# A two-layer graph kernel: layer 1's projection moved ahead of its neighbour sums, edge values 128 and 192, one foreign-value check per four tiles

## The chip, the cores and the metric

The program runs on one core of one Trainium2 chip. The metric is the device time of one execution in microseconds (us). The core has the matrix engine TensorE (PE; its weight loads are listed apart as PEld), the elementwise engines VectorE (DVE) and ScalarE (ACT), GpSimd (POOL, which here issues gathering DMAs) and SyncE (SP, which issues plain DMAs). Each runs its own instruction list in order; semaphores join them. All DMAs share 16 DMA engines.

## The reference

`x` is 8192x128 float32, `adj` is 8192x8192 int32 with values 0 and 1 (about 0.4% ones, symmetric, ones on the diagonal).

```python
def layer0(x, adj, weight, bias):                 # weight is 256x128
    a = adj.astype(x.dtype)
    deg = jnp.sum(a, axis=1, keepdims=True)
    x1 = a @ x / deg
    return jnp.concatenate([x1, x], axis=1) @ weight + bias
def layer1(x, adj, W, a):                         # graph attention
    h = x @ W.T
    e = (h @ a[:128])[:, None] + (h @ a[128:])[None, :]
    return softmax(where(adj == 0, -inf, e), axis=1) @ h
x = layernorm(x + layer0(x, adj, L0_gnn_weight, L0_gnn_bias))
x = layernorm(x + layer1(x, adj, L1_gnn_W, L1_gnn_a))
```

In layer 1 the row term of `e` cancels in the softmax, so the layer is a product of the 0/1 matrix with rows weighted by exp of the column term.

## The kernel before

The adjacency matrix (268 MB) is read once. It comes in 64 tiles of 128 rows, each as two halves of 2 MB, each half as two indirect DMAs that POOL issues (L1144). `adj_in` has three half slots, so half n is asked for when half n-3 has been converted (`load_half`). ACT converts a half from int32 to fp8 (`convert`, L452), DVE transposes it in 32-bit words (`transpose_half`, L751 and L754) into `edgesT` (two tiles deep), and TensorE contracts the tile with all 64 blocks of `x` (`first_layer`: 64 matmuls at L315 with 257 moving columns: a high and a low fp16 part of 128 columns each, and a column of ones for the degree).

Per tile, the sum over neighbours then goes through: DVE divides by the degree (`degree`, `mean_lo`, `mean`), TensorE transposes that mean and the tile of `x` (`transpose_cat`, L579 and L580), ACT copies both to SBUF (`copy_catT`, L458), TensorE multiplies them with the two halves of the 256x128 weight (`project`, L590 and L591), and DVE adds `x + bias` (prepared by POOL, `add_bias`) and normalizes (`residual` to `normed`). The new row tile is transposed (`transpose_x1`, L585) and multiplied with layer 2's weight (`hidden`, L598). In the code the layers are called 0 and 1.

The edges of four tiles are kept, packed as four bits of each byte (`check_and_pack`): tile c of a group of four has its own bit. The same function checks in two halves of 1024 words that no byte holds anything but its edge value (L763). Packed groups are stored to DRAM. From tile 12 on, TensorE also begins layer 2 for the tile at hand over those row blocks whose weighted rows exist already ("bands" of four blocks, `second_layer_inline`): 4(g-1) matmuls with 258 columns for group g. These partial sums are kept in DRAM as well. After tile 63 a second pass loads the packed groups, unpacks one bit per tile (`unpack`) and does the rest of layer 2 (`second_layer`).

The order on each engine is written out by hand: one loop over tiles in each engine's program, with lags (a tile's projection one step behind, its layer norm two behind, its hidden product three behind). Before the loop, `x` is loaded in four quarters by SP and ACT, ACT makes its high part per quarter (L446), DVE the low part (L732), and TensorE starts tile 0 with the first quarter that is there.

Tile numbers below are t = 0 to 63, groups g = t // 4, blocks of `x` in fours j = 0 to 15.

## Time and profile before

| | us |
|---|---|
| median of 3 runs | 1075.53 |
| lowest, highest | 1073.42, 1077.12 |
| the profiled execution | 1073.98 |
| its span in the profile | 1072.3 |

| engine | busy us | share |
|---|---|---|
| PE | 998.3 | 93% |
| PEld | 868.2 | 81% |
| DVE | 728.6 | 68% |
| ACT | 601.0 | 56% |
| POOL | 310.3 | 29% |

The shares are means over stages that differ. In the first half of the span the DMA engines are 90% busy or more in every fortieth of the span, and from then on less and less; PE is at 70 to 80% at first and at 90% or more from the tenth fortieth to the last but one. The mean granted clock of TensorE is 0.993 of full speed.

### The profile page before, as it was taken

The numbers are of one execution on the slowest core, as the hardware profiler recorded it, in microseconds if no ns is written. First come the engines' busy times: TensorE is split into PE (matmuls) and PEld (weight loads), VectorE is DVE, ScalarE is ACT, GpSimd is POOL, SyncE is SP. The second block draws the span as 40 slices with busy tenths as digits, with TensorE's granted clock in tenths as the row PEclk, the third lists the DMA queues.
The fourth block names the chain that finished last, engine by engine and source line by source line (L and its number), as shares of the span: only waits on it lengthen the run. The fifth ranks groups of instructions, "written<-read, shape, count | busy, mean of one in ns | idle before, by whom it ended". The sixth has DMA issues, their size and how long they took to land.

```text
span 1072.3 us, 22059 instructions
## 1 busy us (share of the span) xinstructions
PE 998.3 (93%) x8777; PEld 868.2 (81%) x8777; DVE 728.6 (68%) x1722; ACT 601.0 (56%) x533; POOL 310.3 (29%) x333
## 2 busy tenths in 40 slices
PE   0778888989999999999999999999999999999996
PEld 0566677777888888888888888888888888888885
DVE  4797888888978877777666665555534655656654
...
GB/s 324 422 421 420 402 409 416 416 417 422 407 421 412 417 395 396 385 386 364 357 346 330 336 325 322 318 314 360 83 127 7 19 71 85 85 85 72 26 41 32
DMA packets 51594, 305.36 MB, mean 285 GB/s; under 512 B 6560, under 2 KB 7840, under 8 KB 17952
## 3 DMA queue, kind: packets, MB, share of 16 engines
...
## 4 chain that ended last, share of the span: by engine, by line
PE 81%; DMA 9%; ACT 4%; issue 2%; DVE 2%; POOL 1%; ACTq 0%; DVEq 0%; POOLq 0%
PE ps_agg L315 48%; PE ps_part L315 24%; DMA adj_in<-in_adj_dram,chunk 8%; PE ps_y L315 4%; ACT edges L452 3%; PE ps_y L591 1%; PE ps_y L590 1%; POOL adj_in L1144 1%; DMA x_all<-in_x_dram 1%; PE ps_h L598 1%; DVE edgesT L754 1%; PE ps_catT L579 0%; PE ps_x1T L585 0%; PE ps_catT L580 0%; DVE edgesT L751 0%
## 5 line engine op out<-in xcount | busy, mean ns | idle before, releaser
L315 PE MATMUL ps_agg<-parts,edgesT 128*128 128x257 f16 (+1 forms) x5312 | 616.7, 275 | 34.6 <-DVE edgesT L754 30.9
L315 PEld LDWEIGHTS ps_agg<-parts,edgesT 128*128 128x128 fp8e4 x5312 | 520.6, 98 | 119.2 <-DVE edgesT L754 35.7
L452 ACT ACTIVATE edges<-adj_in 128x4096 fp8e4<-128x4096 int32 x126 | 455.4, 3614 | 32.5 <-DMA adj_in<-in_adj_dram,chunk 31.8
L1144 POOL DMA_INDIRECT adj_in<-in_adj_dram,chunk x256 | 260.9, 1019 | 440.3 <-ACT edges L452 387.5
L315 PE MATMUL ps_part<-parts,edgesT 128*128 128x258 f16 x1664 | 194.6, 273 | 0.0
L315 PEld LDWEIGHTS ps_part<-parts,edgesT 128*128 128x128 fp8e4 x1664 | 162.7, 98 | 22.7
L763 DVE SCALAR_TENSOR_TENSOR stray<-edgesT,stray 128x1024 uint32<-128x1024 uint32 x128 | 158.4, 1238 | 0.5
L522 ACT ACTIVATE std<-mean_var,eps 128x1 f32<-128x1 f32 x64 | 18.9, 295 | 204.0 <-DVE mean_var L977 204.0
L458 ACT ACTIVATE catT<-ps_catT 128x256 f32<-128x256 f32 x64 | 24.6, 384 | 159.2 <-PE ps_catT L580 145.0
L751 DVE STREAM_TRANSPOSE edgesT<-edges 128x512 uint32<-128x512 uint32 x128 | 89.9, 702 | 16.6 <-ACT edges L452 13.4
L315 PE MATMUL ps_part<-parts,packed 128*128 128x258 f16 x836 | 96.4, 273 | 0.0
L315 PEld LDWEIGHTS ps_part<-parts,packed 128*128 128x128 fp8e4 x836 | 81.7, 98 | 11.8
L754 DVE STREAM_TRANSPOSE edgesT<-edges 128x512 uint32<-128x512 uint32 x128 | 85.8, 670 | 3.5 <-ACT edges L487 3.5
L776 DVE SCALAR_TENSOR_TENSOR packed<-edgesT,packed 128x2048 uint32<-128x2048 uint32 (+13 forms) x48 | 73.0, 1521 | 0.0
L825 DVE TENSOR_SCALAR part_lo<-ps_part 128x129 f32<-128x129 f32 x52 | 14.7, 283 | 67.5 <-PE ps_part L315 65.5
L783 DVE RECIPROCAL rcount<-ps_agg 128x1 f32<-128x1 f32 x64 | 10.2, 160 | 60.7 <-PE ps_agg L315 60.6
L1137 POOL TENSOR_TENSOR xb<-x_all,bias 128x128 f32<-128x128 f32 x64 | 47.9, 750 | 1.3
L315 PE MATMUL ps_y<-parts,packed 128*128 128x258 f16 x380 | 45.1, 273 | 0.0
L315 PEld LDWEIGHTS ps_y<-parts,packed 128*128 128x128 fp8e4 x380 | 37.2, 98 | 5.4
L814 DVE RECIPROCAL rstd<-std 128x1 f32<-128x1 f32 x64 | 10.2, 159 | 43.4 <-ACT std L473 43.4
L579 PE MATMUL ps_catT<-ident,agg 128*128 128x128 f32 x64 | 18.2, 285 | 12.8 <-DVE agg L793 11.1
L953 DVE TENSOR_TENSOR part_lo<-ps_agg,adj_in 128x129 f32<-128x129 f32 x26 | 7.6, 291 | 31.4 <-PE ps_agg L315 31.4
...
## 6 DMA issues: line engine op xcount, KB each, us to landing
adj_in<-in_adj_dram,chunk POOLq DMA_INDIRECT x256, 8.8
...
```

Source lines behind the costliest of these rows:

```text
L315: done = eng.matmul(bank[:, 0:cols], rows[:, n // BYTES, n % BYTES, :], moving[:, n, :], start=(n == first), stop=(n == last))
L452: act.activation(edges[:, half, :, :], adj_in[:, n % SLOTS, :, :], ACT.Copy, scale=2.0 if t % GROUP == GROUP - 1 else 1.0, saturate=False) ...
L458: act.activation(catT[:, :], ps_catT[:, 0:2 * P], ACT.Copy).then_inc(s_catTc, 1)
L522: act.activation(std[:, u % 2:u % 2 + 1], mean_var[:, u % 2, 1:2], ACT.Sqrt, bias=eps[:, :])\
L579: pe.transpose(ps_catT[:, 0:P], agg[:, t % 2, :], ident[:, :])
L751: dve.transpose(dst[:, 2 * half], src[:, 0])
L754: dve.transpose(dst[:, 2 * half + 1], src[:, 1]).then_inc(s_trh, 1)
L763: dve.scalar_tensor_tensor(stray[:, :], edgesT[:, t % 2, part * width:(part + 1) * width], every_byte(0xFF ^ EDGE[c]), stray[:, :], ALU.bi ...
L776: dve.scalar_tensor_tensor(word, bits, every_byte(BIT[c]), word, ALU.bitwise_and, ALU.bitwise_or).then_inc(s_pack, 1)
L825: dve.tensor_scalar(part_lo[:, :], ps_part[:, LO:LO + HCOLS], BIT_SCALE[c], None, ALU.mult)\
L1137: pool.tensor_tensor(xb[:, t % 4, :], x_all[:, t, :], bias[:, :], ALU.add).then_inc(s_xb, 1)
L1144: pool.indirect_dma_start(adj_in[:, n % SLOTS, r, :], None, adj_chunks, bass.IndirectOffsetOnAxis(chunk[:, 0:1], 0), element_offset=first_ ...
```

## The change

Layer 1's projection is linear, so it can be applied to `x` before the neighbour sums. Now u = x @ W[0:128] is made first for all 64 blocks, in 16 groups of four: TensorE transposes four blocks (`transpose_x`), ACT copies them (`copy_xT`), TensorE multiplies them (`dense`), ACT and DVE split the result into the high and the low fp16 part (`split_u`, `split_u_lo`). Tile 0's contraction waits for all 16 (`s_lo0`). The contraction is then over u, so its quotient by the degree is already the projected mean.

The other half, v = x @ (W[128:256] + I) + bias, takes in the residual too (`w0_self`). It is made for two groups ahead of the loop (`dense_self`) and for the other 14 at odd tiles 1 to 27 (`late_transpose_x`, `copy_late_xT`, `late_dense_self`), and DVE writes it over `x_all` (`keep_v`). Per tile, `residual_lo` and `residual` then give the row before its norm directly, without a transpose or a product; its lag goes from two steps to one. `transpose_cat`, `copy_catT`, `project` and POOL's `add_bias` are gone.

Edges are converted to 128 in the first three tiles of a group and to 192 in the fourth, and `KEPT` and `FOREIGN` are masks of their fp8 bytes. Packing keeps a tile's own bit and all bits that an edge never has, at the full 2048 words for every group (before, later groups packed fewer words); the check then reads the packed words once per group instead of every tile. The fourth tile's bit is unpacked with a shift and a mask in one instruction. The four chunks of tile 0 are converted inside the loop over the 16 groups, after steps 11, 13, 15 and 16 (`FIRST_AFTER`), and POOL's first adjacency loads wait for the third quarter of `x` instead of the second.

```diff
-    EDGE = [0x38, 0x38, 0x38, 0x40]
-    BIT = [0x08, 0x10, 0x20, 0x40]
-    BIT_SCALE = [2.0 ** -6, 2.0 ** -5, 2.0 ** -3, 1.0]
+    EDGE = [128.0, 128.0, 128.0, 192.0]
+    KEPT = [0x10, 0x20, 0x40, 0x04]
+    FOREIGN = 0x8B
+    UNPACKED = [2.0 ** -5, 2.0 ** -3, 2.0, 2.0 ** -6]
+    BIT_SCALE = [bit / edge for bit, edge in zip(UNPACKED, EDGE)]
...
+        FIRST_AFTER = [11, 13, 15, 16]
+        AHEAD = 2
+        def late_group(t):
+            j = (t + 3) // 2
+            return j if t % 2 == 1 and AHEAD <= j < GROUPS else None
...
+            def copy_xT(j):
+                act.wait_ge(s_xT, j + 1)
+                if 0 <= j - 2 < AHEAD:
+                    act.wait_ge(s_v, j - 1)
+                wait(act, s_u, j - 1)
+                act.activation(xT[:, j % 2, :, :].rearrange("p c i -> p (c i)"), ps_xT[j % 2][:, :], ACT.Copy)\
+                    .then_inc(s_xTc, 1)
+            def split_u(j):
+                act.wait_ge(s_u, j + 1)
+                act.activation(parts0[:, GROUP * j:GROUP * (j + 1), 0:F],
+                               ps_u[j % 2][:, :].rearrange("p (c f) -> p c f", c=GROUP), ACT.Copy, scale=XSCALE)\
+                    .then_inc(s_hi0, 1)
...
+            for j in range(GROUPS + 1):
+                if j < GROUPS:
+                    copy_xT(j)
+                if j > 0:
+                    split_u(j - 1)
+                if j in FIRST_AFTER:
+                    convert_first(FIRST_AFTER.index(j))
...
-                if on(t, 1):
-                    copy_catT(t - 1)
                 if on(t, 3):
                     copy_x1T(t - 3)
+                if late_group(t) is not None:
+                    copy_late_xT(late_group(t))
...
-                if on(t, 2):
-                    deviation(t - 2)
+                if on(t, 1):
+                    deviation(t - 1)
...
+            def dense(j):
+                pe.wait_ge(s_xTc, j + 1)
+                wait(pe, s_lo0, j - 1)
+                for c in range(GROUP):
+                    last = pe.matmul(ps_u[j % 2][:, c * F:(c + 1) * F], xT[:, j % 2, c, :], w0_sb[:, 0, :],
+                                     start=True, stop=True)
+                last.then_inc(s_u, 1)
...
+            def dense_self(j):
...
+                for c in range(GROUP):
+                    last = pe.matmul(ps_v[j][:, c * F:(c + 1) * F], xT[:, j, c, :], w0_self[:, :],
+                                     start=True, stop=True)
+                last.then_inc(s_v, 1)
...
+            def late_dense_self(j):
+                pe.wait_ge(s_xTlc, j - AHEAD + 1)
+                pe.wait_ge(s_vkept, j)
...
             def first_layer(t):
...
-                wait(pe, s_aggr, t - 1)
...
+                if t == 0:
+                    pe.wait_ge(s_lo0, GROUPS)
+                if t == 1:
+                    pe.wait_ge(s_vkept, AHEAD)
+                contract(pe, ps_agg[t % 2], edgesT[:, t % 2, :], parts0[:, :, 0:2 * F + 1],
+                         range(NBLK), 0, NBLK - 1).then_inc(s_agg, 1)
...
             for t in range(TILES):
-                if on(t, 1):
-                    transpose_cat(t - 1)
                 if on(t, 3):
                     transpose_x1(t - 3)
+                if late_group(t) is not None:
+                    late_transpose_x(late_group(t))
                 first_layer(t)
-                if on(t, 1):
-                    project(t - 1)
                 if on(t, 3):
                     hidden(t - 3)
+                if late_group(t) is not None:
+                    late_dense_self(late_group(t))
                 if inline(t):
                     second_layer_inline(t)
...
-            pe.wait_ge(s_aggr, TILES - 1)
-            second_layer(0, range(0, 16))
-            transpose_cat(TILES - 1)
+            pe.wait_ge(s_z, TILES - 1)
             transpose_x1(TILES - 3)
-            second_layer(0, range(16, 36))
-            project(TILES - 1)
+            second_layer(0, range(0, 8))
             hidden(TILES - 3)
             transpose_x1(TILES - 2)
-            second_layer(0, range(36, READY))
+            second_layer(0, range(8, 16))
             hidden(TILES - 2)
+            transpose_x1(TILES - 1)
+            second_layer(0, range(16, 24))
+            hidden(TILES - 1)
+            second_layer(0, range(24, READY))
...
+            pe.wait_ge(s_z, TILES)
+            second_layer(1, range(0, READY))
...
+            def keep_v(j):
+                dve.wait_ge(s_v, j + 1)
+                if j == 0:
+                    dve.wait_ge(s_bias, 16)
+                dve.tensor_tensor(x_all[:, GROUP * j:GROUP * (j + 1), :],
+                                  (ps_v[j] if j < AHEAD else ps_v_late)[:, :].rearrange("p (c f) -> p c f", c=GROUP),
+                                  bias[:, :].rearrange("p (o f) -> p o f", o=1).to_broadcast([P, GROUP, F]),
+                                  ALU.add).then_inc(s_vkept, 1)
...
-            def check_and_pack(t):
+                words_transposed(t, 2 * half)
...
-                width = TW // CHECKS
-                def check(part):
-                    wait(dve, s_check, CHECKS * t + part)
-                    dve.scalar_tensor_tensor(stray[:, :], edgesT[:, t % 2, part * width:(part + 1) * width],
-                                             every_byte(0xFF ^ EDGE[c]), stray[:, :],
-                                             ALU.bitwise_and, ALU.bitwise_or).then_inc(s_check, 1)
-                check(0)
-                words = slice(bands_of(g) * P, TW)
-                bits = edgesT[:, t % 2, words]
-                word = packed[:, g % 2, words]
+                bits, word = edgesT[:, t % 2, :], packed[:, g % 2, :]
                 if c == 0:
                     wait(dve, s_pkst, 16 * (g - 1))
...
+                    wait(dve, s_check, CHECKS * (g - 1))
+                    dve.tensor_single_scalar(word, bits, every_byte(KEPT[c] | FOREIGN), ALU.bitwise_and)\
+                        .then_inc(s_pack, 1)
                 else:
                     dve.wait_ge(s_pack, t)
-                    dve.scalar_tensor_tensor(word, bits, every_byte(BIT[c]), word, ALU.bitwise_and,
+                    dve.scalar_tensor_tensor(word, bits, every_byte(KEPT[c] | FOREIGN), word, ALU.bitwise_and,
                                              ALU.bitwise_or).then_inc(s_pack, 1)
-                check(1)
+            def check(g, part):
+                width = TW // CHECKS
+                dve.wait_ge(s_pack, GROUP * (g + 1))
+                wait(dve, s_check, CHECKS * g + part)
+                dve.scalar_tensor_tensor(stray[:, :], packed[:, g % 2, part * width:(part + 1) * width],
+                                         every_byte(FOREIGN), stray[:, :],
+                                         ALU.bitwise_and, ALU.bitwise_or).then_inc(s_check, 1)
...
+            def residual_lo(t):
                 dve.wait_ge(s_rdeg, t + 1)
...
+                dve.scalar_tensor_tensor(agg_lo[:, 0:F], ps_agg[t % 2][:, LO:LO + F], rcount[:, :], x_all[:, t, :],
+                                         ALU.mult, ALU.add).then_inc(s_aglo, 1)
+            def residual(t):
                 dve.wait_ge(s_aglo, t + 1)
...
+                dve.scalar_tensor_tensor(z[:, t % 2, :], ps_agg[t % 2][:, 0:F], rcount[:, :], agg_lo[:, 0:F],
+                                         ALU.mult, ALU.add).then_inc(s_z, 1)
...
-                if t in (1, 3, 5, 7):
-                    extremes(t // 2)
+                if t in (40, 44, 48, 52):
+                    extremes(t // 4 - 10)
...
+                if c < 3:
+                    dve.tensor_single_scalar(words_of_turn[u % 4][:, words], source[:, words], every_byte(KEPT[c]),
+                                             ALU.bitwise_and).then_inc(s_unp, 1)
+                else:
+                    dve.tensor_scalar(words_of_turn[u % 4][:, words], source[:, words], 1, every_byte(KEPT[c] << 1),
+                                      ALU.logical_shift_left, ALU.bitwise_and).then_inc(s_unp, 1)
...
-            pool.wait_ge(s_x[1], 16 * NQ)
-            for n in range(SLOTS):
+            pool.wait_ge(s_x[2], 16 * NQ)
+            for n in range(2 * TILES):
                 load_half(n)
```

TensorE's list ahead of and around tile 0, before. `ps_small` receives layer 2's weight, transposed.

```order
L563 MATMUL ps_small<-ident,w_sb 128x128
L564 MATMUL ps_small<-a_sb,w_sb 128x1
L315 MATMUL ps_agg<-parts,edgesT 128x257 x64
L579 MATMUL ps_catT<-ident,agg 128x128
L580 MATMUL ps_catT<-ident,x_all 128x128
```

The same place in the changed kernel, from the last three groups of u on (`partial` here holds the copied transposes; `ps_y` and `ps_h` hold u).

```order
L632 MATMUL ps_catT<-ident,x_all 128x128 x4
L639 MATMUL ps_h<-w_sb,partial 128x128 x4
L632 MATMUL ps_x1T<-ident,x_all 128x128 x4
L639 MATMUL ps_y<-w_sb,partial 128x128 x4
L639 MATMUL ps_h<-w_sb,partial 128x128 x4
L676 MATMUL ps_small<-ident,w_sb 128x128
L677 MATMUL ps_small<-a_sb,w_sb 128x1
L345 MATMUL ps_agg<-parts,edgesT 128x257 x64
L654 MATMUL ps_catT<-ident,x_all 128x128 x4
```

Sixteen steps of four transposes and four float32 products now stand ahead of tile 0 (two of them with four products more, for v), and the transposes for a late group behind it.

ACT's list before its first full conversion, before.

```order
L446 ACT_TABLE_LOAD
L446 ACTIVATE parts<-x_all 128x16x128 x4
L487 ACTIVATE edges<-adj_in 128x2048 x4
L490 ACTIVATE w1T<-ps_small 128x129
L452 ACTIVATE edges<-adj_in 128x4096 x2
```

The end of that part in the changed kernel; L542 converts a chunk of tile 0, L512 is the first half of tile 1.

```order
L504 ACTIVATE parts0<-ps_y 128x4x128 [waits u_done]
L542 ACTIVATE edges<-adj_in 128x2048 [waits first_tile_landed1]
L499 ACTIVATE partial<-ps_catT 128x512 [waits u_done,xT_done]
L504 ACTIVATE parts0<-ps_h 128x4x128 [waits u_done]
L499 ACTIVATE partial<-ps_x1T 128x512 [waits u_done,xT_done]
L504 ACTIVATE parts0<-ps_y 128x4x128 [waits u_done]
L542 ACTIVATE edges<-adj_in 128x2048 [waits first_tile_landed2]
L504 ACTIVATE parts0<-ps_h 128x4x128 [waits u_done]
L542 ACTIVATE edges<-adj_in 128x2048 [waits first_tile_landed3]
L554 ACTIVATE w1T<-ps_small 128x129
L512 ACTIVATE edges<-adj_in 128x4096 [waits half_transposed,adj_landed2]
```

The conversions of tile 0, which free the slots that POOL waits for, now stand behind copies that wait for TensorE.

TensorE's list for a tile in the later part of the loop, before (a tile with 11 bands, then the start of the next).

```order
L590 MATMUL ps_y<-w_sb,catT 128x128
L591 MATMUL ps_y<-w_sb,catT 128x128
L598 MATMUL ps_h<-w1T,x1T 128x129
L315 MATMUL ps_part<-parts,edgesT 128x258 x44
L579 MATMUL ps_catT<-ident,agg 128x128
L580 MATMUL ps_catT<-ident,x_all 128x128
L585 MATMUL ps_x1T<-ident,x_all 128x128
L315 MATMUL ps_agg<-parts,edgesT 128x257 x64
```

The same in the changed kernel, over the step from 10 to 11 bands.

```order
L699 MATMUL ps_h<-w1T,x1T 128x129
L345 MATMUL ps_part<-parts,edgesT 128x258 x40
L692 MATMUL ps_x1T<-ident,x_all 128x128
L345 MATMUL ps_agg<-parts,edgesT 128x257 x64
L699 MATMUL ps_h<-w1T,x1T 128x129
L345 MATMUL ps_part<-parts,edgesT 128x258 x44
```

Two transposes and two float32 products of each tile are gone from TensorE there.

## Rows read from the trace of the kernel before

**Rows 1.** Busy time by stage (us; PEclk, DMA share and GB/s last).
```profile
0.00:26.80 26.80, 0.66 (x3) 0.61 (x3) 11.49 (x7) 14.45 (x8) 15.29 (x23) 1.00 0.97 323
54.00:302.50 248.50, 216.45 (x1844) 183.52 (x1844) 213.99 (x398) 203.29 (x159) 119.96 (x115) 0.99 1.01 415
378.00:423.40 45.40, 45.40 (x406) 40.03 (x407) 34.64 (x73) 35.34 (x29) 18.23 (x21) 1.00 0.99 391
423.40:789.40 366.00, 366.00 (x3276) 323.23 (x3274) 226.42 (x501) 240.06 (x194) 110.74 (x129) 1.00 0.83 316
813.10:1072.30 259.20, 250.91 (x2243) 218.92 (x2241) 151.13 (x573) 22.40 (x76) 0.00 (x0) 0.99 0.17 54
```
**Rows 2.** Chain that ended last: start us, us, what; starts of six contractions.
```profile
65.08 7.35 PE ps_agg L315 x64
...
302.53 7.33 PE ps_agg L315 x64
...
334.08 7.34 PE ps_agg L315 x64
...
423.44 7.16 PE ps_agg L315 x64
...
789.37 1.79 PE ps_agg L315 x16
...
813.06 7.16 PE ps_y L315 x64
```
**Rows 3.** Timeline of PE over one late tile: start us, us, instruction.
```profile
745.93 0.27 PE L579 MATMUL ps_catT<-ident,agg 128*128 128x128 f32 x1
...
746.15 0.27 PE L585 MATMUL ps_x1T<-ident,x_all 128*128 128x128 f32 x1
746.26 7.32 PE L315 MATMUL ps_agg<-parts,edgesT 128*128 128x257 f16 x64
753.42 0.38 PE L590 MATMUL ps_y<-w_sb,catT 128*128 128x128 f32 x2
...
753.87 0.39 PE L598 MATMUL ps_h<-w1T,x1T 128*128 128x129 f32 x2
754.09 6.43 PE L315 MATMUL ps_part<-parts,edgesT 128*128 128x258 f16 x56
```
**Rows 4.** Timeline of the first 40 us; idle time and releaser in brackets.
```profile
7.08 1.28 ACT L446 ACT_TABLE_LOAD   x1 [7.08 <-DMA x_all<-in_x_dram]
...
16.72 1.91 ACT L446 ACTIVATE parts<-x_all 128x2048 f16<-128x2048 f32 x1 [1.00 <-DMA x_all<-in_x_dram]
...
27.59 1.91 ACT L487 ACTIVATE edges<-adj_in 128x2048 fp8e4<-128x2048 int32 x1 [0.57 <-DMA adj_in<-in_adj_dram,chunk]
...
30.30 10.18 PE L315 MATMUL ps_agg<-parts,edgesT 128*128 128x257 f16 x64 [11.78 <-DVE edgesT L754]
```
**Rows 5.** The same chain in its first 34 us.
```profile
3.32 10.46 DMA x_all<-in_x_dram
...
16.76 2.40 issue
19.16 8.40 DMA adj_in<-in_adj_dram,chunk
```
**Rows 6.** Groups of instructions by shape: busy us, mean ns | idle before.
```profile
L452 ACT ACTIVATE edges<-adj_in 128x4096 fp8e4<-128x4096 int32 x126 | 455.4, 3614 | 32.5 <-DMA adj_in<-in_adj_dram,chunk 31.8 <-issue 0.3
L763 DVE SCALAR_TENSOR_TENSOR stray<-edgesT,stray 128x1024 uint32<-128x1024 uint32 x128 | 158.4, 1238 | 0.5
L458 ACT ACTIVATE catT<-ps_catT 128x256 f32<-128x256 f32 x64 | 24.6, 384 | 159.2 <-PE ps_catT L580 145.0 <-issue 14.3
L776 DVE SCALAR_TENSOR_TENSOR packed<-edgesT,packed 128x2048 uint32<-128x2048 uint32 x9 | 22.1, 2458 | 0.0
L463 ACT ACTIVATE x1T<-ps_x1T 128x128 f32<-128x128 f32 x64 | 17.4, 272 | 2.0 <-PE ps_x1T L585 2.0
```
**Rows 7.** PE alone in 42 to 48 us: busy, PEclk, DMA share, GB/s.
```profile
42.00:48.00 6.00, 5.27 (x33) 0.72 1.02 422
```

279 lines of the change are left out of this document (150 added, 129 removed).

## The prediction

> **What bounds the kernel now.** I read the busy times by stage first, then the chain that ended last for the starts of the tiles, then the timeline of one late tile and of the first 40 us. The stages show two limits [rows 1]. From 54 to 302.5 us the DMA share is 1.01 at 415 GB/s while PE is busy for 216 of 248 us: the matrix comes in no faster. From 378 us PE is busy without a gap (45.4 of 45.4, then 366 of 366 us) and the DMA share falls to 0.99 and 0.83: there every PE instruction that goes away shortens the run. The last stage, from 813 us, is PE again, in code that the change hardly touches.
>
> The chain gives the tiles' starts [rows 2]: tile 3 at 65.08, tile 25 at 302.53, tile 28 at 334.08, tile 36 at 423.44, the end of tile 63 at 789.37. Tiles 3 to 25 took 10.79 us each (237.45 / 22), tiles 25 to 27 10.52 each, which I take as the DMA's period; tiles 28 to 35 took 11.17 each.
>
> **The steady part: what goes from TensorE.** In a late tile [rows 3] the two transposes that go stand from 745.93 to 746.15, 0.22 us, and the two products of the projection from 753.42 to 753.87, 0.45 us: 0.67 us per tile. The transpose and product for the hidden rows stay. The v products that come in cost four transposes (0.11 each) and four float32 products (0.225 each), 1.34 us at each odd tile from 1 to 27, or 0.67 per tile: up to tile 27 TensorE's work is thus what it was, inside a DMA-bound stretch; from tile 28 it is less.
>
> Tiles 36 to 63: 28 x 0.67 = 18.8 us, all of it on the chain. Tiles 28 to 35: TensorE would need 11.17 - 0.67 = 10.5, just the DMA's period. With stores of packed groups in the same queue (391 GB/s were moved there at 11.3 us per tile [rows 1], so about 4.4 MB per tile, 10.6 us at 419) I take 10.6: 8 x (11.17 - 10.6) = 4.6 us. At the end of the loop the last tile's transposes and projection go (0.67) and some 0.1 to 0.5 us of a wait for them: 0.8. Sum of the gains: 24.2 us.
>
> **What else changes in the loop.** DVE loses 128 checks of 1.24 us (158 us, rows 6) and gets 32 of them back (40 us). Packing at full width costs 2.46 us where narrower groups took less; for the last groups that is up to 2 us more per tile. DVE is busy 226 of 366 us in tiles 36 to 63 [rows 1], or 8.1 of 13.1 us per tile, and loses about as much as it gains there, so this lies beside TensorE. ACT loses a 0.38 us copy per tile. The norm's step is one tile earlier, and ACT's second conversion of a tile stands behind its square root, which waits for DVE's moments, which wait for the sums of the tile before the last transposed one. From those sums on, DVE's row steps (some 1.5 us), the root, a conversion of 3.61 us [rows 6] and two word transposes are about 7 us; TensorE still has more than a tile's 7.3 us contraction ahead of it. Its cover is thin only where PE is not behind, and there the DMA sets the pace. All this I cost at 0; uncovered, it is rival D. The two-operation unpacking of every fourth tile is at most doubled, some 1.2 us more on a DVE that is busy 151 of 259 us [rows 1]: 0.
>
> **The new part ahead of tile 0.** Before, TensorE waits until 30.30 for tile 0 [rows 4], and the adjacency has been streaming since 19 us at the latest [rows 5]. Now every step j costs TensorE 0.44 us of transposes and 0.90 of products at full clock, twice that at 1.2 GHz, and ACT two copies of 512 columns: 272 ns at 128 columns and 384 at 256 [rows 6] give 0.272 + 3 x 0.112 = 0.61 us each. The engines overlap (two banks for each product), so a step costs about 1.38 us at full clock.
>
> Which clock? Tile 0 took 10.18 us for 64 matmuls [rows 4] where a late tile takes 7.32 [rows 3]. The 2.86 us lost mean 5.7 us at half speed, after idling. And after the idle time at 40 us the granted clock is 0.72 on average over 42 to 48 us [rows 7]. So I count about 6 us of 1.2 GHz from the landing of the first quarter at 7.1 us [rows 4], in which steps 0 and 1 pass with their v products, and then full clock. That puts the products of step 3 at 17.7 and, at 1.38 per step, those of step 10 at 27.2. From there the four chunk conversions of tile 0 (1.91 us each, rows 4) stand in ACT's list between the copies and stretch the steps: they end at about 29.7, 33.8, 37.9 and 40.4 us. Tile 0's contraction starts near 41 us, and since TensorE has idled by then it takes 10 us again.
>
> A late tile 0 is no cost in itself; the DMA queue running dry is. POOL asks for half 3 when the second chunk is converted, for half 4 at the fourth, for half 5 and 6 after the conversions of tile 1. Three halves (6.3 MB), x (4.2) and the rest make 10.8 MB; 8.7 MB moved by 26.8 us [rows 1], the other 2.1 MB take 5 us, so the queue was fed up to 31.8 us. The dead time between the issue and a moving transfer is 2.40 us in the chain [rows 5], with 0.2 for POOL 2.6. The gaps are then:
> - at the start, since the first loads wait for x's third quarter: 1.0 us (2.5 us of x are left to cover 3.5 of issue and dead time), so the queue is empty at 32.8;
> - half 3: 33.8 + 2.6 - 32.8 = 3.6 us, done at 41.4;
> - half 4: 40.4 + 2.6 - 41.4 = 1.6 us;
> - half 5 and 6 come in time; half 7 waits for the first half of tile 2, whose conversion stands behind the copy of the late transposes, and these behind tile 0 on TensorE: 0.7 us.
>
> That is 6.9 us. Lost DMA time is not won back before tile 36, since the DMA is the limit up to there. Bounds: 0 if the steps are hidden behind the loads, about 25 if each step runs in series; the value nearest to the rows is that of overlapping steps, and I take 6.9.
>
> The Trainium skill ("DMA: Bandwidth & Descriptors", section Anatomy of one DMA) gives a lone GpSimd DMA a fixed cost of 2.0 us. By that figure the three later restarts would be 0.4 us shorter each and the sum 1.2 us lower; no row before shows a restart from an empty queue, so the trace neither confirms nor denies it.
>
> **Sum.** The profiled execution took 1073.98 us, 1.7 more than its span, and 1.55 less than the median of 1075.53. 1073.98 - 24.2 + 6.9 = 1056.7; I say 1057 us.
>
> **Rivals.**
> - A, TensorE stays at 1.2 GHz through all 16 steps. For it: the clock is low after short idle times [rows 7]. Against it: at that clock TensorE is the slowest of the three and works without a pause, and tile 0 rose to full speed under continuous work. A step is then 2.64 us; step 10's products end at 39, the second chunk is converted at 47, the fourth at 55. The gaps grow by 14.5 us: 1071.
> - B, slower: each step runs in series, because TensorE's product waits for ACT's copy and ACT's split for the product. At full clock 0.44 + 0.61 + 0.90 + 0.61 and some 0.6 for four hand-overs are 3.2 us. The second chunk is then converted at 7.1 + 14 x 3.2 + 3.8 = 56 instead of 33.8, the gaps grow by 22 us: 1079. It decides against the change once that conversion ends later than 51 us (33.8 + 17.3). Against it: a copy for step j stands ahead of the split of step j-1 in ACT's list, and TensorE's transposes for j ahead of the products for j-1.
> - C, more is won: DVE is busy 214 of 248 us in the DMA-bound stretch [rows 1], and tiles 3 to 25 took 0.27 us longer than the period of 10.52. If DVE's checks were behind that, their going gives up to 22 x 0.27 = 6 us: 1051. Against it: the DMA share is 1.01, which leaves no idle time to win.
> - D, it does not do what it says: with DVE's steps in another order, tiles 36 to 63 wait for the transposed words by what TensorE saved. 1056.7 + 18.8 = 1075.5. Against it: 5 us of DVE are idle per tile.
>
> **How the numbers follow.** Forecast 0.55, A 0.15, B 0.08, C 0.14, D 0.05, others 0.03. A measurement of this kernel tells about 0.3% (3.2 us) from no change. The forecast, C, half of A and a little of the rest are faster: 0.81; half of A and D are no change: 0.10; B and a little more are slower: 0.09. The likeliest case alone spans 1051 to 1064 (gaps of 1 to 14 us). The range reaches down to C with 2 us to spare and up past A: 1049 to 1073.
>
> **What would show it.** In the changed profile: TensorE's products for u packed 1.4 us apart after 14 us, or 2.6 (A) or 3.2 (B); tile 0 starting near 41 us; the DMA share falling below 1 between 32 and 44 us and nowhere else ahead of tile 36; a period of 10.5 to 10.6 us up to tile 36 and then 7.5 us plus 0.45 per band, so that tiles 36 to 63 take 347 us and not 366 (D: 366); no wait of TensorE for the transposed words after tile 36. The prediction is wrong if the gaps at the start exceed 14 us, or if the saved TensorE time reappears as waits in the loop.

## The result, and the profile after

The changed kernel takes 1068.0 us (median of 5 runs, 1065.95 to 1069.11) against 1075.53 before: 7.5 us less, ratio 0.9935 [0.9916, 0.9954]. Run again later it took 1068.84 us beside 1074.77, ratio 0.9947 [0.9929, 0.9966]. The forecast was 1057: faster as foretold, but by less than half.

The page of the changed kernel: VectorE is busy 59 us less, TensorE 4.5 us more.

```profile
PE 1002.8 (94%) x8769; PEld 873.2 (82%) x8769; DVE 669.3 (63%) x1591; ACT 598.4 (56%) x512; POOL 251.4 (24%) x269
```

Busy time by stage in the changed kernel (columns as in [rows 1]):

```profile
0.00:26.80 26.80, 17.20 (x121) 16.25 (x122) 7.17 (x11) 10.64 (x19) 7.26 (x19) 1.00 0.92 299
26.80:54.00 27.20, 20.63 (x157) 17.73 (x156) 13.54 (x20) 22.57 (x23) 8.10 (x8) 0.87 0.77 286
54.00:302.50 248.50, 216.64 (x1822) 185.33 (x1821) 170.81 (x339) 200.04 (x141) 89.11 (x90) 0.95 1.01 410
378.00:423.40 45.40, 43.91 (x391) 38.10 (x390) 32.29 (x67) 34.64 (x26) 17.33 (x18) 1.00 1.01 413
423.40:789.40 366.00, 364.52 (x3257) 319.27 (x3255) 235.11 (x464) 245.18 (x183) 101.04 (x107) 1.00 0.87 333
813.10:1066.30 253.20, 244.88 (x2189) 213.66 (x2187) 145.93 (x554) 20.60 (x71) 0.00 (x0) 0.99 0.17 55
```

The third row is the one to look at. Its DMA share is the same 1.01 as before, but it moved 410 GB/s and not 415, at a clock of 0.95 and not 0.99. That stage was to stay as it was.

The best view for a kernel made of equal tiles is the start of each tile's contraction in TensorE's timeline, set against the kernel before. How much later a tile starts than before, in us (one profiled execution each; further rows are those of the experiments):

| kernel | tile 0 | tile 4 | tile 28 | tile 36 | tile 63 | growth 4 to 28 |
|---|---|---|---|---|---|---|
| changed | 14.0 | 8.5 | 13.9 | 11.7 | -5.3 | 5.4 |
| the same again (c1) | 14.8 | 9.6 | 14.4 | 12.2 | -4.8 | 4.8 |
| e5 loads earlier | 16.2 | 10.5 | 14.8 | 12.5 | -4.5 | 4.3 |
| e6 bias early | 19.1 | 13.6 | 17.7 | 15.4 | -1.6 | 4.1 |
| e8 x whole | 15.3 | 10.1 | 14.2 | 14.7 | -2.3 | 4.0 |
| e13 v kept later | 16.9 | 11.6 | 19.4 | 17.1 | 0.1 | 7.8 |
| e12 fill behind six tiles | 15.4 | 9.7 | 15.0 | 12.8 | -4.2 | 5.3 |
| e4 fill behind four tiles | 15.5 | 9.6 | 10.6 | 8.8 | -8.2 | 1.0 |
| e3 chunks early | 15.4 | 7.3 | 9.0 | 6.7 | -10.2 | 1.6 |
| e1 half 1 back | 15.2 | 11.4 | 12.2 | 9.1 | -8.9 | 0.8 |
| e2 hi rows later | 16.7 | 11.2 | 11.5 | 9.3 | -8.7 | 0.4 |
| e14 both orders | 15.4 | 10.5 | 11.5 | 8.5 | -9.5 | 1.1 |
| e10 start and ScalarE | 22.3 | 16.2 | 17.4 | 14.3 | -3.7 | 1.2 |
| e15 four edits | 15.9 | 8.5 | 9.3 | 5.4 | -12.6 | 0.8 |
| e16 four and fill | 15.1 | 7.7 | 8.9 | 4.8 | -13.2 | 1.3 |

In the changed kernel 8.5 us are lost by tile 4, 5.4 more by tile 28; then 2.2 are won up to tile 36, 17.0 up to tile 63 and 0.7 behind it: 6.0 between the two profiled executions (1073.98 and 1068.0). The late tiles come within 1 us of what was foretold; the start and the middle don't. (Of e13 and e16 the profiled execution was the longest of its kernel, of e3, e4 and e15 the shortest; the medians below tell how far to trust a row.)

**The start.** Its timeline in the changed kernel, by engine:

```profile
9.67 1.12 PE L632 MATMUL ps_x1T<-ident,x_all 128*128 128x128 f32 x4 [4.92 <-DMA x_all<-in_x_dram]
...
20.06 1.13 PE L639 MATMUL ps_h<-w_sb,partial 128*128 128x128 f32 x8 [0.85 <-DVE parts L831]
21.46 1.06 PE L639 MATMUL ps_y<-w_sb,partial 128*128 128x128 f32 x8
...
22.79 1.06 PE L639 MATMUL ps_h<-w_sb,partial 128*128 128x128 f32 x8
```

From 20 to 31 us the steps follow each other by 1.33 us (1.38 was forecast). But the first quarter of `x` is there at 9.67, not 7.1, and step 3 (steps are counted from 0) waits 0.85 us for VectorE, which has waited for the bias. ScalarE finishes the second chunk at 37.06 and the fourth at 43.48 (33.8 and 40.4 forecast). The DMA windows around it (the last three columns are the clock, the DMA share and GB/s):

```profile
32.00:34.00 2.00, 0.79 (x7) 0.56 (x6) 0.78 (x2) 2.00 (x4) 0.00 (x0) 1.00 0.63 262
34.00:36.00 2.00, 2.00 (x20) 2.00 (x19) 1.33 (x2) 1.73 (x3) 0.00 (x0) 1.00 0.03 12
36.00:38.00 2.00, 0.79 (x7) 0.55 (x6) 0.71 (x1) 2.00 (x4) 0.67 (x1) 1.00 0.02 4
38.00:40.00 2.00, 1.85 (x17) 1.69 (x17) 1.27 (x2) 1.73 (x4) 1.20 (x2) 1.00 0.55 78
40.00:42.00 2.00, 0.26 (x4) 0.18 (x2) 0.90 (x3) 2.00 (x3) 0.00 (x0) 1.00 0.94 373
42.00:50.00 8.00, 5.72 (x28) 4.07 (x29) 4.48 (x7) 8.00 (x4) 4.36 (x4) 0.57 0.95 320
```

From 32 to 42 us 1.46 MB were moved, 3.5 us of work at 419 GB/s: 6.5 us are lost. From 42 to 50 it is 1.9 us, and 24 GB/s less over the first 26.8 us are 1.5 us. Sum 9.9, where tile 3 starts 9.5 late.

**The middle.** The chain that ended last, in the changed kernel, from one load to another that it delays:

```profile
209.99 12.52 DMA adj_in<-in_adj_dram,chunk
...
222.53 3.63 ACT edges L512
...
226.82 0.68 DVE edgesT L853
...
227.55 8.81 PE ps_agg L345 x64
...
237.47 1.34 PE ps_part L345 x12
238.81 0.11 PE ps_x1T L692
238.92 7.16 PE ps_agg L345 x64
...
247.76 0.45 PE ps_catT L654 x4
...
248.23 0.02 ACT xT_late L491
...
248.72 3.62 ACT edges L512
...
252.60 1.05 POOL adj_in L1261
```

The stage is not bound by the DMA alone. The chain goes through two contractions, since ScalarE's list has the copies of TensorE's transposes ahead of the next conversion, and the next load waits for that conversion. TensorE's side of it:

```profile
223.68 0.60 PE L654 MATMUL ps_catT<-ident,x_all 128*128 128x128 f32 x4
227.55 8.81 PE L345 MATMUL ps_agg<-parts,edgesT 128*128 128x257 f16 x64 [3.27 <-DVE edgesT L853]
```

TensorE idles for 3.27 us, its clock falls, and the contraction takes 8.81 us where 7.33 is usual. What comes of it in ScalarE's timeline and in the windows:

```profile
238.96 0.28 ACT L518 ACTIVATE x1T<-ps_x1T 128x128 f32<-128x128 f32 x1 [2.06 <-PE ps_x1T L692]
239.13 3.61 ACT L512 ACTIVATE edges<-adj_in 128x4096 fp8e4<-128x4096 int32 x1
```
```profile
220.00:224.00 4.00, 4.00 (x38) 3.59 (x36) 2.41 (x6) 3.41 (x4) 1.87 (x2) 1.00 1.03 421
228.00:230.00 2.00, 2.00 (x11) 1.42 (x10) 1.83 (x6) 2.00 (x1) 0.60 (x1) 0.50 1.08 389
238.00:240.00 2.00, 2.00 (x21) 1.76 (x19) 1.79 (x7) 1.04 (x2) 0.84 (x1) 1.00 0.91 328
```

A clock of 0.50 at 228 us is the lower of the two levels. At 238 the DMA moves 328 GB/s with a share of 0.91. Idle times of 2.5 to 4.6 us ahead of a contraction stand in this trace at 65, 97, 139, 162, 183, 227 and 272 us, most of them ahead of tiles 4g + 1; the slow contractions (8.7 to 10.1 us) follow all but the first. In the kernel before the longest idle time of this kind between 60 and 340 us is 1.8 us, and two contractions there take 8.97.

What is new behind a group's end shows in ScalarE's groups: its high part of the weighted rows waits for VectorE 9 times, 10.0 us in sum (0.8 us in the kernel before), and the next conversion stands behind it.

```profile
L537 ACT ACTIVATE parts<-h_row 128x516 f16<-128x516 f32 x16 | 10.2, 638 | 10.1 <-DVE h_row L951 10.0
```

TensorE's waits for transposed words go on behind this stage. These are the contractions of tiles 29, 33 and 37:

```profile
360.02 7.34 PE L345 MATMUL ps_agg<-parts,edgesT 128*128 128x257 f16 x64 [1.70 <-DVE edgesT L853]
403.03 7.33 PE L345 MATMUL ps_agg<-parts,edgesT 128*128 128x257 f16 x64 [1.25 <-DVE edgesT L853]
446.93 7.33 PE L345 MATMUL ps_agg<-parts,edgesT 128*128 128x257 f16 x64 [0.77 <-DVE edgesT L853]
```

### The profile page after: what moved, and what is told of

It reads as the page before. It is cut to its first block, busy times and chain, and to the rows that moved or that the text cites. A ratio compares the mean times of both kernels' runs of the same rounds, so it can differ in the third digit from the quotient of the medians.

```text
span 1066.3 us, 21633 instructions
## 1 busy us (share of the span) xinstructions
PE 1002.8 (94%) x8769; PEld 873.2 (82%) x8769; DVE 669.3 (63%) x1591; ACT 598.4 (56%) x512; POOL 251.4 (24%) x269
## 4 chain that ended last, share of the span: by engine, by line
PE 70%; ACT 12%; DMA 9%; issue 5%; DVE 2%; POOL 1%; ACTq 1%; DVEq 0%
PE ps_agg L345 40%; PE ps_part L345 23%; ACT edges L512 9%; DMA adj_in<-in_adj_dram,chunk 8%; PE ps_y L345 4%; DMA bias<-in_L_gnn_bias_dram 1%; DVE edgesT L853 1%; PE ps_h L699 1%; POOL adj_in L1261 1%; ACT L528 1%; ACT L533 1%; PE ps_y L639 1%; ACT edges L542 0%; ACTq L477 0%; PE ps_x1T L692 0%
## 5 line engine op out<-in xcount | busy, mean ns | idle before, releaser
L512 ACT ACTIVATE edges<-adj_in 128x4096 fp8e4<-128x4096 int32 x126 | 454.6, 3609 | 33.6 <-DMA adj_in<-in_adj_dram,chunk 33.5
L1261 POOL DMA_INDIRECT adj_in<-in_adj_dram,chunk x256 | 249.9, 976 | 496.3 <-ACT edges L512 422.7
L853 DVE STREAM_TRANSPOSE edgesT<-edges 128x512 uint32<-128x512 uint32 x256 | 166.8, 689 | 141.8 <-ACT edges L512 137.5
L345 PEld LDWEIGHTS ps_part<-parts,edgesT 128*128 128x128 fp8e4 x1664 | 162.7, 98 | 22.7
L882 DVE SCALAR_TENSOR_TENSOR packed<-edgesT,packed 128x2048 uint32<-128x2048 uint32 x48 | 109.5, 2282 | 0.0
L518 ACT ACTIVATE x1T<-ps_x1T 128x128 f32<-128x128 f32 x64 | 17.6, 275 | 138.6 <-PE ps_x1T L692 138.6
L889 DVE SCALAR_TENSOR_TENSOR stray<-packed,stray 128x1024 uint32<-128x1024 uint32 x32 | 39.0, 1218 | 0.0
L932 DVE TENSOR_SCALAR part_lo<-ps_part 128x129 f32<-128x129 f32 x52 | 15.1, 290 | 37.3 <-PE ps_part L345 36.8
L699 PE MATMUL ps_h<-w1T,x1T 128*128 128x129 f32 x128 | 24.7, 275 | 0.7 <-ACT x1T L518 0.7
L910 DVE SCALAR_TENSOR_TENSOR z<-ps_agg,rcount,agg_lo 128x128 f32<-128x128 f32 x64 | 22.5, 351 | 2.3
L902 DVE SCALAR_TENSOR_TENSOR agg_lo<-ps_agg,rcount,x_all 128x128 f32<-128x128 f32 x64 | 22.5, 351 | 2.3
L925 DVE TENSOR_SCALAR x_all<-z,mean_var,rstd 128x128 f32<-128x128 f32 x64 | 22.2, 347 | 2.3
```

The source lines that it names most:

```text
L345: done = eng.matmul(bank[:, 0:cols], rows[:, n // BYTES, n % BYTES, :], moving[:, n, :], start=(n == first), stop=(n == last))
L512: act.activation(edges[:, half, :, :], adj_in[:, n % SLOTS, :, :], ACT.Copy, scale=EDGE[t % GROUP], saturate=False).then_inc(s_conv, 1)
L518: act.activation(x1T[:, :], ps_x1T[:, 0:P], ACT.Copy).then_inc(s_x1Tc, 1)
L699: pe.matmul(ps_h[:, 0:HCOLS], x1T[:, :], w1T[:, 0:HCOLS], start=True, stop=True).then_inc(s_h, 1)
L853: return dve.transpose(dst[:, r], src)
L882: dve.scalar_tensor_tensor(word, bits, every_byte(KEPT[c] | FOREIGN), word, ALU.bitwise_and, ALU.bitwise_or).then_inc(s_pack, 1)
```

## The experiments

Theory S: the start is priced by the moments at which the second and the fourth chunk are converted. Theory 1: the order around a group's end uses up the lead in the middle. VectorE now transposes both halves of a tile before it makes the weighted rows, which is new; ScalarE's part of these rows stands ahead of a conversion, which it did before as well. Theory 2: the lower clock after TensorE's idle times is what costs there. Theory 3: the copies, transposes and products for v at odd tiles cost it.

**e1: VectorE's second half goes back behind the weighted rows.**

```diff
                 if on(t, 0) and t > 0:
                     transpose_half(t, 0)
-                    transpose_half(t, 1)
...
                     if t == weighted_at(g):
                         weighted(g)
+                if on(t, 0) and t > 0:
+                    transpose_half(t, 1)
```

> The changed kernel with one line moved on DVE: the second half of a tile is again transposed behind the weighting of a finished group (weighted), as before, and no longer ahead of it. Theory 1 (DVE's order makes ACT wait at every group's end, so a slot of adj_in is freed late and the DMA stream thins out): ACT's waits for h_row (9 times, 10.0 us) go, tiles 12 to 28 start 170 to 172 us apart in sum and not 176.1, and the median falls by 4 to 6 us, to 1062 to 1064. Theory 2 (TensorE's clock falls after the longer idle times before tiles 4g+1, and those tiles take 8.7 to 10.1 us and not 7.3): no change, 1068. Theory 3 (the loss is the copy, transposes and products for v at odd tiles): no change, 1068.

1065.29 us (1064.26 to 1067.39), ratio to before 0.9908 [0.989, 0.9925]. The growth from tile 4 to tile 28 falls from about 5 to 0.8 us, and ScalarE's wait for the weighted rows from 10.0 to 0.8 us. Tiles 12 to 28 took 173.5 us, less of a gain than the 170 to 172 expected, and the time is 1.3 us above the expected range.

**e2: ScalarE's weighted rows behind the conversion.**

```diff
-                for g in range(GROUPS - 1):
-                    if t == weighted_at(g):
-                        weighted_hi(g)
                 if on(t + 1, 0):
                     convert(t + 1, 0)
+                for g in range(GROUPS - 1):
+                    if t == weighted_at(g):
+                        weighted_hi(g)
```

> The changed kernel with one block moved on ACT: the high part of the weighted rows (weighted_hi) is made behind the first conversion of the next tile, not ahead of it; DVE's order is that of the change. Theory 1: ACT's wait for the weighted rows falls into a time in which they are long made, tiles 12 to 28 take 170 to 173 us, the median is 1063 to 1065. Theories 2 and 3: 1068.

1065.43 us (1062.04 to 1071.35), ratio 0.9911 [0.9884, 0.9938]; growth 0.4 us, tiles 12 to 28 in 171.1 us, ScalarE's wait 0.8 us. This edit restores nothing: it is an order that neither kernel had. The work for v is in both e1 and e2 as it was, so theory 3 is not borne out.

**e3: chunks of tile 0 converted earlier.**

```diff
-        FIRST_AFTER = [11, 13, 15, 16]
+        FIRST_AFTER = [6, 8, 10, 12]
```

> The changed kernel with the four chunks of tile 0 converted after steps 6, 8, 10 and 12 instead of 11, 13, 15 and 16. If the hole in the DMA stream from 33 to 41 us is due to when the second and fourth chunk are converted (37.1 and 43.5 us), they are now converted at about 31 and 40 us, the two holes shrink from 8.7 us in sum to about 6, and the median falls by 2 to 3 us to 1065 or 1066. If later stages make good what the start loses, it falls by under 1 us.

1066.74 us (1063.76 to 1067.63), ratio 0.9915 [0.9896, 0.9933]: 1.3 to 2.1 us less than the changed kernel in its two measurements, where 2 to 3 were expected. The second chunk is done at 31.6 and the fourth at 39.9, but tile 4 starts only 1.2 us earlier: half 5 now waits 6.46 us for tile 1's first conversion, which stands behind all steps, and a hole opens at 48 us.

**e4: TensorE kept busy behind tiles 12, 16, 20 and 24.**

```diff
+                if t in (12, 16, 20, 24):
+                    contract(pe, ps_small, edgesT[:, t % 2, :], parts0[:, :, 0:2 * F + 1], range(16), 0, 15)
```

> The changed kernel with 16 more matmuls (1.8 us at full clock) on TensorE in tiles 12, 16, 20 and 24, into a bank that nobody reads, ahead of the idle time after which the clock falls. Theory 2: contractions 13, 17, 21 and 25 take 7.3 us and not up to 10.1, tiles 12 to 28 take 4 to 6 us less, the median is 1062 to 1064. Theories 1 and 3: the contractions may be shorter, but ACT and the DMA set the pace: 1067 to 1069.

1066.12 us (1065.67 to 1068.01), ratio 0.9917 [0.99, 0.9933]; in its trace no idle time above 2 us and no slow contraction after 173 us; growth 1.0 us, tiles 12 to 28 in 170.8 us. ScalarE's wait for the weighted rows is still there, 10.1 us in sum. The trace is as theory 2 foretold, the time lies between the two forecasts. More work on TensorE, and nothing slower.

**c1 and e5: the changed kernel again, and its loads let go at x's second quarter.**

```diff
-            pool.wait_ge(s_x[2], 16 * NQ)
+            pool.wait_ge(s_x[1], 16 * NQ)
```

> The changed kernel itself, once more, as the yardstick of this call, and for a second profile of it. The experiments so far left their loop alone or moved one block, and all took 171 to 173 us from tile 12 to 28 where the first profile of the change has 176.1. If that was the change's own, it is again 175 to 177 us; if it was chance of one execution, it is 170 to 173. The median should be 1066 to 1069.

> The changed kernel with POOL's first adjacency loads behind the second quarter of x again, as before, and not the third. The prediction added up the holes in the DMA stream, so by it the one at 16 to 19 us (about 2 us) is won back: 2 us faster. Theory S (only the times at which the second and the fourth chunk of tile 0 are converted count, because they release the next loads): the queue runs dry 2 us earlier and the hole from 33 us on grows by as much; no change, or 0.5 us slower since x lands later.

1068.84 us (1066.07 to 1071.75) and 1068.92 (1064.81 to 1074.72), ratios 0.9947 [0.9929, 0.9966] and 0.9953 [0.9934, 0.9971]. Tiles 12 to 28 took 175.1 us in c1: the loss is the change's own and no chance of one execution. In e5 the first load went out at 13.3 and not 14.8 to 15.8 us, but the products of step 3 waited 2.19 us (1.59 in c1) and the second chunk was done at 39.3: nothing was won by the hole closed at the front. This agrees with theory S.

**e8: x without its separate first blocks.** Their four DMAs fall away, and the weight goes behind the first quarter.

```diff
-            for a in (2, 3):
-                act.dma_start(x_all[QUAD * a:QUAD * (a + 1), 0:BYTES, :].rearrange("p c f -> p (c f)"),
-                              x_quarters[0, a][:, 0, :]).then_inc(s_xfirst, 16)
-            act.dma_start(w0_sb[:, :, :], w0.rearrange("(c p) f -> p c f", p=P)).then_inc(s_const, 16)
...
-                    first = 1 if s == 0 else 0
+                    first = 0
```

> The changed kernel with the first quarter of x in one piece per 32 rows again (no DMAs for its first block ahead), and the weight behind it. If the late landing of that quarter (9.7 us instead of 7.1) is due to the six DMAs put ahead of it, it lands at 7.1 to 8 us, the chunks are converted 1.5 to 2.5 us earlier and so are all tiles: 1 to 2 us faster. If TensorE's work at the low clock sets the start, the time is the same.

1068.89 us (1066.85 to 1071.59), ratio 0.9948 [0.993, 0.9966]. The first quarter is there at 7.03 us, as the forecast had it, but the products of step 3 then wait 3.67 us for VectorE, which waits for the bias, and the second chunk is done at 38.4. The first blocks' DMAs are neither the gain nor the delay.

**e6: the bias asked for early; e13: needed later.** e6 moves the DMA; e13 leaves it and moves VectorE's first two copies of v:

```diff
             act.dma_start(w0_sb[:, :, :], w0.rearrange("(c p) f -> p c f", p=P)).then_inc(s_const, 16)
+            act.dma_start(bias[:, :], b0.rearrange("(o f) -> o f", o=1).to_broadcast([P, F])).then_inc(s_bias, 16)
```
```diff
-                if 0 < j <= AHEAD:
-                    keep_v(j - 1)
+                if 6 < j <= 6 + AHEAD:
+                    keep_v(j - 7)
```

> The changed kernel with the bias asked for right behind w0 instead of behind x's last quarter, so that VectorE's first copy of v does not wait for it (it waited 4.26 us in the changed kernel, and the split of step 3 behind it held TensorE up for 0.85). If the start is priced by when the second and fourth chunk are converted: both about 0.9 us earlier (36.2 and 42.6 instead of 37.1 and 43.5), 1067.2 where the changed kernel takes 1068.0 to 1068.8. Rival: step 3 then waits as long for x itself, no gain, 1068 to 1069.

> The changed kernel with VectorE's first two copies of v (which need the bias) moved from steps 1 and 2 to steps 7 and 8. No DMA moves. If the wait for the bias held the steps up: none of TensorE's products for u waits at step 3, tile 0 starts 1 to 3 us earlier (near 42.5), the second and fourth chunk are converted near 36 and 42, and the time is 1066 to 1067.5. Rival: the steps then wait for x itself, nothing changes, 1068 to 1069.

e6: 1072.27 us (1067.9 to 1077.47), ratio 0.9973 [0.9954, 0.9992]. Slower than the changed kernel: with this DMA of 64 KB, the same 512 bytes for each of 128 partitions, ahead of it x came later: TensorE's second transposes, the first that need the whole quarter, start at 11.48, and the first load goes out at 18.26. e13: 1070.09 us (1068.33 to 1074.02), ratio 0.9949 [0.9929, 0.9969], no gain. The wait of step 3 is gone, but a pause of 2.7 us comes at step 6, and in e6 one of 2.65. Both expectations failed: the wait for the bias stands in the traces, but nothing is won by taking it away.

**e7: the kernel before with the checks alone** (edges 128 and 192, packing at full width, one check per group; its order and its projection stay).

```diff
-                    check_and_pack(t)
+                    pack(t)
+                if on(t, 1) and (t - 1) % GROUP == GROUP - 1:
+                    check((t - 1) // GROUP, 0)
+                if on(t, 2) and (t - 2) % GROUP == GROUP - 1:
+                    check((t - 2) // GROUP, 1)
```

> The kernel before with one part of the change alone: edges 128 and 192, packing at full width, one check per group on the packed words; the projection, all orders and the start are those of before. If DVE's checks held up the DMA-bound stretch (rival C of the prediction), tiles 3 to 28 take 263 to 265 us instead of 269.0 and the median falls by 3 to 5 us. If DVE was no limit there, 1074 to 1076: no change.

1072.46 us (1070.58 to 1077.35), ratio 0.9978 [0.9959, 0.9997]. Tile 4 starts 2.1 us earlier than before, and tile 63 2.3 earlier: the 158.4 us of checks [rows 6] were in the way, if for 2 us only, and nearly all of it ahead of tile 4. Tiles 3 to 28 took 268.3 us where 263 to 265 were expected.

```profile
L777 DVE SCALAR_TENSOR_TENSOR stray<-packed,stray 128x1024 uint32<-128x1024 uint32 x32 | 43.2, 1349 | 0.0
```

**e9: the kernel before with both halves transposed first.** The reverse of e1, in the other kernel.

```diff
                     transpose_half(t, 0)
+                    transpose_half(t, 1)
...
                         weighted(g)
-                if on(t, 0):
-                    transpose_half(t, 1)
```

> The kernel before with one edit: VectorE transposes both halves of a tile's words at the head of its step, as the changed kernel does. Theory 2 (TensorE's idle time ahead of the first tile after a group's end is what costs, since the clock falls after it): the idle time there grows from 1.8 to 2.5 to 3.1 us, one to three contractions between tiles 12 and 28 take 8.7 us or more, those 16 tiles take 172 to 175 us instead of 170.4, and the time is 1076 to 1079. Rival (the order of the halves is harmless): 170.4 and 1074 to 1075.

1099.82 us (1099.09 to 1101.33), ratio 1.0231 [1.0201, 1.0262]: 25 us slower, where 1 to 4 were expected. Here the same order also puts the mean behind both transposes, and TensorE's next instruction is that mean's transpose. VectorE, at the head of its step, waits for ScalarE's conversions, 127.4 us in sum where the kernel before has 13.4. From the waits, and one of them in TensorE's timeline:

```profile
DVE edgesT L751 <- ACT edges L452: 127.4, 61, 3.7
PE ps_catT L579 <- DVE agg L793: 53.1, 29, 4.1
```
```profile
181.55 0.47 PE L579 MATMUL ps_catT<-ident,agg 128*128 128x128 f32 x1 [3.23 <-DVE agg L793]
```

The middle of e9 is the plainest case of what the DMA share does not tell: 0.99, with 390 GB/s.

```profile
54.00:302.50 248.50, 209.59 (x1722) 177.21 (x1720) 196.85 (x369) 188.99 (x148) 98.43 (x108) 0.95 0.99 390
```

**e12: TensorE kept busy behind tiles 4 to 24** (e4 with two places more, in ps_part).

```diff
+                if t in (4, 8):
+                    contract(pe, ps_part, edgesT[:, t % 2, :], parts0[:, :, 0:2 * F + 1], range(16), 0, 15)
```

> The changed kernel with 16 more matmuls (1.8 us, their sums are not used) behind tiles 4, 8, 12, 16, 20 and 24, ahead of TensorE's waits of 2.6 to 4.6 us. It leaves ScalarE's and VectorE's lists as they are. Theory 2 (the clock): no contraction after 90 us above 8.5 us, tiles 3 to 12 take 96.5 instead of 97.3, tiles 12 to 28 take 170.5 instead of 176, the time is 1061 to 1065. Theory 1 (ScalarE waits for VectorE's weighted rows and converts late, whatever TensorE's clock): 175 and 1068.

1067.05 us (1066.28 to 1070.79), ratio 0.9929 [0.9904, 0.9954]. The expectation failed: idle times of 2.9 to 4.0 us stayed at 99, 142, 164 and 187 us, with slow contractions behind them, and the growth was 5.3 us. A fill of 1.8 us does not cover a wait of 4; why the same fill behind tile 12 sufficed in e4 and not here is not shown.

**e10: e2 and e3 with the bias early and tile 1's first half converted after step 14.**

```diff
                     convert_first(FIRST_AFTER.index(j))
+                if j == 14:
+                    convert(1, 0)
...
-                if on(t + 1, 0):
+                if t > 0 and on(t + 1, 0):
                     convert(t + 1, 0)
```

> The changed kernel with four edits: the chunks of tile 0 converted after steps 6, 8, 10 and 12, tile 1's first half converted after step 14 instead of after all steps, the bias asked for early, and ScalarE's weighted rows behind the conversion. If the start is priced by the DMA queue's holes, the hole at 48 to 52 us (half 5, which waited 6.5 us for tile 1's first half) goes too: tile 3 starts near 70 instead of 75, tiles 12 to 28 take 171, the time is 1056 to 1061. Rival (what is won at the start is given back up to tile 28, as with the loads asked for early): 1064 to 1066.

1069.6 us (1067.71 to 1075.84), ratio 0.9951 [0.993, 0.9972]. The growth is 1.2 us, small as in e2, but the expected 1056 to 1061 us are missed: tile 0 starts at 52.64. The hole at 48 us is filled and one opens from 64 to 70, where half 7 waits for tile 2's conversion and that for the copy of transposes behind tile 0. The bias alone accounts for some 4 us of it (e6).

**e14: e1 and e2 together; e15: also e3 and e13's edit; e16: also e4's.** The edits are those shown above. Of the two orders that the expectations call "put back" only VectorE's was the kernel's before.

> The changed kernel with both orders of the loop put back: the second half's word transpose behind the weighted rows on VectorE, and the weighted rows behind the conversion on ScalarE. If either edit gives back one and the same lead: like each alone, 1065 to 1066, and tiles 4 to 28 no slower than before (offset growing by under 1.5 us). If they are two: 1063.

> Both orders of the loop put back, the chunks converted after steps 6, 8, 10 and 12, and v kept after step 6. If the start's holes and the loop's loss are separate: 1065 less 3 for the chunks less 1 to 3 for the bias, 1059 to 1062, tile 28 about 5 us behind the kernel before instead of 14. Rival (tile 0's own start limits, as where tile 1's half was converted ahead): 1063 to 1065.

> The four edits and 16 more matmuls, whose sums are not used, behind tiles 12, 16, 20 and 24. If the clock costs time of its own beside the orders: 0.5 to 2 us less than with the four edits alone. If it cost only where the orders had used up the lead: the same within 0.5 us.

| kernel | median us | lowest to highest | ratio to before |
|---|---|---|---|
| e14 | 1064.1 | 1063.82 to 1071.27 | 0.9907 [0.9876, 0.9938] |
| e15 | 1062.11 | 1060.95 to 1063.31 | 0.9877 [0.9853, 0.9901] |
| e16 | 1059.79 | 1059.28 to 1060.86 | 0.9854 [0.983, 0.9877] |

e14 is like each edit alone (0.9908, 0.9911) within their intervals: it is one lead, and either edit gives it back. e15 adds the start, 2.0 us in the median, but tile 28 is 9.3 us behind where about 5 was expected. e16 is 2.3 us below e15 in the median, with no overlap of their times, and in its trace TensorE idles nowhere for 2 us or more after 139 us (the window cuts the first and the last of these rows):

```profile
222.76 1.06 PE L345 MATMUL ps_part<-parts,edgesT 128*128 128x258 f16 x8
223.65 0.27 PE L692 MATMUL ps_x1T<-ident,x_all 128*128 128x128 f32 x1
223.76 0.60 PE L654 MATMUL ps_catT<-ident,x_all 128*128 128x128 f32 x4
225.84 0.40 PE L345 MATMUL ps_agg<-parts,edgesT 128*128 128x257 f16 x2 [1.48 <-DVE edgesT L855]
```
```profile
54.00:302.50 248.50, 220.24 (x1900) 189.50 (x1901) 176.06 (x351) 203.12 (x143) 88.67 (x93) 0.98 1.01 417
```

417 GB/s in the middle stage, against 410 in the changed kernel and 415 before. e16 is faster than both kernels. Against c1's interval of the ratio (0.9929 to 0.9966) those of e1, e15 and e16 lie apart; those of e2, e3, e4 and e14 overlap it by 0.001 or less. Against that of the first measurement (0.9916 to 0.9954) only e15 and e16 lie apart.

## Why the prediction was wrong

The terms, forecast and as measured in the two profiled executions:

| term | forecast | measured |
|---|---|---|
| holes at the start (by tile 4) | +6.9 | +8.5 |
| the loop's orders, tiles 4 to 28 | 0 | +5.4 |
| tiles 28 to 35 | -4.6 | -2.2 |
| tiles 36 to 63 (measured: the 27 from start to start) | -18.8 | -17.0 |
| the loop's end | -0.8 | -0.7 |
| sum | -17.3 | -6.0 |

- **The step that failed** is "All this I cost at 0", with the reason that the cover "is thin only where PE is not behind, and there the DMA sets the pace". It is 5.4 of the 11.3 us missed up to tile 28 (4.8 in c1), and part of what is missing behind it. The prediction followed the steps of an ordinary tile; what cost was the tile behind a group's end, where VectorE's new order delays the weighted rows and ScalarE's conversion waits behind them. The DMA share of 1.01 [rows 1] was read as a DMA at its limit, and rival C was turned down by the same reading. The share stood at 1.01 or 0.99 with 415, 410, 417 and 390 GB/s: a share at 1 does not tell that no more can be moved. The Trainium skill ("Perfetto Trace Analysis", section Identifying the Most-Contended Engine) calls the occupancy of the DMA engines misleading and goes by the use of the memory's bandwidth; these runs agree, with 390 to 417 GB/s at a share of 0.99 to 1.01. In that stage load, conversion, transposes and contraction form a ring with three slots; in the chain above two contractions and their copies delay a load.
- **What the runs showed in its place.** Runs with the order of e1 or e2 grew by 0.4 to 1.3 us in the middle (e1, e2, e10, e14, e15, e16), those without by 4.0 to 7.8 (changed, c1, e5, e6, e8, e12, e13), but for e3 (1.6) and e4 (1.0). Between 60 and 340 us ScalarE waited 5.4 to 7.4 us for the weighted rows in every run with the changed kernel's order, e3 and e4 too, and at most 0.1 us in those with e1's or e2's. From tile 4 to tile 63, e1, e2 and e14 gained 19.9 to 20.3 us on the kernel before, the changed kernel 13.8 and c1 14.5; the terms of the forecast for these tiles give 22.7. That the order costs is shown by this and by the times. In e3 and e4 the wait stands and the growth is small, so the wait alone does not fix it; why e3's trace loses only 1.6 us is not shown. No run put VectorE's whole old order back, and what the missing 2.4 to 2.8 us of the 22.7 are is not shown either.
- **The clock** (theory 2) has a share: e4 left both orders alone and lost 1.0 us in the middle of its trace, and e16 gains 2.3 us on e15. e12 speaks against it as the sole cause. The experiments don't part it from the order: between tiles 12 and 28 the changed kernel has three slow contractions, 4.4 us over 7.33 each in sum, e1 and e14 have one and e2 none. In e1 the idle times ahead of tiles 17 and 21 are still 2.8 and 3.0 us, but the contractions behind them take 7.34. How the 5 us divide between late words and slow contractions stays open, and single executions of the changed kernel differ by up to 6 us (1065.95 to 1071.75).
- **Holes at the start:** the mechanism was right, the sizes too small. The hole ahead of half 3 was priced at 3.6 us and was 6.5. The second chunk came at 37.06 and not at 33.8. In this trace x's first quarter came 2.6 us later than assumed, an arrival read off a kernel that does not load the quarter's first blocks apart. But that is not the cause alone: in e8 the quarter came at 7.03, and in c1 at 8.59, and the second chunk still only at 38.4 and 37.9. Nor was it right that "a late tile 0 is no cost in itself": in e10 it reopened the hole further on. What holds TensorE's steps for 1 to 4 us between 17 and 28 us, in the trace of each run with the steps (0.85 us in the changed kernel's first), is known in part: at step 3 it is the bias, but with the bias out of the way (e6, e13, e15) a pause comes at a later step. Its cause stays open.
- **Tiles 28 to 35** took 86.95 us, or 10.87 each, and not 10.6. TensorE waited 3.2 us of them for transposed words, 1.70 ahead of tile 29 and 1.25 ahead of tile 33 (0.17 us in the kernel before); without these waits it is 10.47 each, TensorE's own need as forecast. The same 3.2 us stand in c1, e3, e5, e6, e12 and e13, which are late by 9.0 to 19.4 us at tile 28, so it is the lists and not the lateness. In e2 it is 3.1 us, in e1 and e14 2.1, in e15 1.5 and in e16 1.2 (these two gain 3.9 and 4.2 us of the 4.6), so the orders account for a part of it. The DMA's period as a limit does not show there.
- **Tiles 36 to 63** were right within 1 us. 27 of them took 334.85 us, 17.0 less, and in e1, e2 and e14 333.85, or 18.0: 27 x 0.67 = 18.1. The 1.0 us between them is the order again: the prediction said "no wait of TensorE for the transposed words after tile 36", and there is one, 0.77 us ahead of tile 37, which e1, e2 and e14 don't have. D is refuted in its size, and so are A (the steps ran 1.33 us apart) and B.
- **Rival C** was right that the checks cost something, not where: they alone gave 2.1 us by tile 4 and 2.3 in all (e7). From tile 3 to tile 28, the stretch of its 6 us, it was 0.7.
- The restart of an empty queue was priced at 2.6 us. The load issued at 37.33 moves nothing up to 38.9 and 213 GB/s from 38.9 to 39.4, so the first packets start some 1.6 us after the issue; by the 78 GB/s over 38 to 40 us (19% of 419), full traffic from about 39.6 would have moved as much, an estimate of 2.3 us. The Trainium skill ("DMA: Bandwidth & Descriptors", section Anatomy of one DMA) gives a fixed cost of 2.0 us for a GpSimd DMA; this trace does not decide between the two prices, and 0.3 us a hole were not what was missed.
